# Dynamic convolution's three engine orders laid out anew, and residual tiles loaded and summed beside the sweeps, in a four-layer float32 kernel

## The reference, cut to what matters

```python
x = x + L0(gn(x))   # dynamic 3x3 convolution: mean -> hidden -> softmax gives 4 weights, which mix 4 experts per sample
x = x + L1(gn(x))   # four sweeps (down, up, right, left): row += relu(conv1d(previous row)), 9 taps
x = x + L2(gn(x))   # linear attention with rotation, plus a 3x3 depthwise convolution of a view of the input
x = x + L3(gn(x))   # four sweeps again
```

## Time and profile before

| | us |
|---|---|
| median of 3 runs | 3129.11 |
| the profiled execution | 3132.45 |
| its span | 3130.7 |
| stage one | 0 to 428 |
| first layer's sweeps | 428 to 1339 |
| local stage | 1339 to 1583 |
| attention | 1583 to 2118 |
| third layer's sweeps, final sum | 2118 to 3130.7 |

### The profile page before, as it was taken

One profiled execution on the slowest core, in us unless ns is written; L12 is line 12 of the kernel. 1 busy time (PEld: TensorE's weight loads), 2 busy tenths in 40 slices (PEclk: granted clock), 3 DMA queues, 4 the chain that ended last, 5 costly groups with the idle time before them and its releaser, 6 DMA issues. The chain is left out here.

```text
span 3130.7 us, 71818 instructions
## 1 busy us (share of the span) xinstructions
PE 2747.3 (88%) x25712; PEld 2482.8 (79%) x25712; DVE 2172.1 (69%) x5174; ACT 1363.0 (44%) x2113; POOL 288.4 (9%) x801
## 2 busy tenths in 40 slices
PE   5888879999999999917969998878999999999791
PEld 3666669999999999913447777758999999999791
DVE  7888846666666666687018888886666666666865
ACT  3766642246632222236436666643225662222120
POOL 1112110000000000045000101010000000000602
PEclk9899989999999999958979999998999999999795
DMA  4334230000000000087054877856000000000758
GB/s 89 81 90 99 67 124 0 0 0 0 0 0 0 0 0 0 0 233 198 1 87 73 120 104 102 116 73 107 0 0 0 0 0 0 0 0 0 121 94 127
DMA packets 735622, 164.89 MB, mean 53 GB/s; under 512 B 728209, under 2 KB 728849, under 8 KB 730641
## 3 DMA queue, kind: packets, MB, share of 16 engines
q1 hardware_dynamic: 608928, 136.86, 22.7%
q10 hardware_dynamic: 126576, 26.41, 5.4%
HBM read 96.13 MB, written 67.11 MB: 52 GB/s over the span
## 5 line engine op out<-in xcount | busy, mean ns | idle before, releaser
L269 PE MATMUL L_conv<-L_x_hi,L_w_hi 128*128 128x256 f32 x5040 | 1251.0, 283 | 46.5 <-DVE L_w_lo L236 28.7
L269 PE MATMUL L_conv<-L_x_hi,L_w_lo 128*128 128x256 f32 x5040 | 1249.5, 283 | 0.0
L156 ACT ACTIVATE L_row_b<-S,L_bias 128x256 f32 (+1 forms) x1008 | 514.2, 510 | 1168.9 <-DVE L_x_hi L210 1158.0
L269 PEld LDWEIGHTS L_conv<-L_x_hi,L_w_hi 128*128 128x128 f32 x5040 | 958.7, 190 | 49.5 <-issue 28.9
L269 PEld LDWEIGHTS L_conv<-L_x_hi,L_w_lo 128*128 128x128 f32 x5040 | 957.0, 190 | 0.0
L220 DVE SCALAR_TENSOR_TENSOR S<-L_conv,L_neg_bias,L_row_b 128x256 f32 x1008 | 487.7, 484 | 517.5 <-PE L_conv L273 516.7
L273 PE MATMUL L_conv<-L_x_lo,L_w_hi 128*128 128x256 f32 x5040 | 771.3, 284 | 4.9 <-DVE L_x_lo L212 4.8
L273 PEld LDWEIGHTS L_conv<-L_x_lo,L_w_hi 128*128 128x128 f32 x5040 | 677.7, 190 | 7.4 <-DVE L_x_lo L212 7.4
L212 DVE TENSOR_TENSOR L_x_lo<-S,L_x_hi 128x256 fp32r<-128x256 f32 x1016 | 455.3, 448 | 34.7
L210 DVE TENSOR_SCALAR L_x_hi<-S 128x256 fp32r (+1 forms) x1016 | 316.7, 312 | 35.3
L604 PE MATMUL dc_conv<-dc_xz_hi,dc_w_hi 128*128 128x512 f32 x384 | 171.3, 446 | 6.5 <-DVE dc_w_lo L731 6.5
(11 more groups left out here) (177 smaller groups left out, 2896.4 us busy)
## 6 DMA issues: line engine op xcount, KB each, us to landing
dc_raw<-x SPq DMA_DIRECT2D x32, 512.0 KB, 6.6
x_scratch<-dc_raw SPq DMA_DIRECT2D x16, 1024.0 KB, 7.4
lp_xr<-x_scratch SPq DMA_DIRECT2D x16, 1024.0 KB, 7.0
x_scratch<-lp_xr SPq DMA_DIRECT2D x32, 512.0 KB, 7.7
at_res<-x_scratch SPq DMA_DIRECT2D x32, 512.0 KB, 10.5
x_scratch<-at_res SPq DMA_DIRECT2D x64, 256.0 KB, 5.3
fs_buf<-x_scratch SPq DMA_DIRECT2D x32, 512.0 KB, 6.7
at_G<-x_scratch ACTq DMA_DIRECT2D x56, 256.0 KB, 5.8
```

Source lines behind the costliest of these rows:

```text
L156: nc.scalar.activation(row_b[p][:, :, :], line(k, at_step(k, i), p), ACT.Identity, bias=bias[:, k:k + 1]).then_inc(row_b_ready[p], 1)
L269: nc.tensor.matmul(out, w[:, k, s * P:(s + 1) * P], x_hi[p][:, s:s + J, :], start=(s == 0 and n == 0), stop=False)
```

## The change

Stage one: the orders of TensorE, ScalarE and VectorE in a sample. TensorE does chunk 0 first, then the input group; the hidden product stands behind two thirds of chunk 1, the logits behind a third of chunk 2. VectorE makes the low input of a sample's second part in that sample's own turn, and the first part's behind the mixing weights; the first expert's share is made by ScalarE (`first_expert`). ScalarE's moves into S are issued one by one, the fourth of them two samples late. `beff` has two buffers. The experts' loads move from ScalarE's queue to SP's, behind the first image. At the start mixing is done ahead of the low inputs.

Beside the sweeps: the tiles of the ring now live through sweeps, local stage and attention, where they are G, the rotations, one turned tile and the constants (class `Shared`). SP loads five of them beside the first layer's sweeps. Within the last sweep GpSimd adds three of four quarters of the columns, and VectorE takes their statistics, one between the halves of a step. The local stage adds and measures the fourth quarter of these five samples. The bands are loaded at the start of the local stage, from ScalarE's queue, and waited for in four parts. x2 has the layout [16, 128, 2048] and is stored in one DMA per sample; attention's residual loads become four DMAs for two. Attention's constants and its first two G are loaded by SP at the end of the local stage; of G only the pad columns are set to one. The diff, cut to its core:

```diff
-                with dve.Fori(0, STEPS) as i:
-                    for p in range(2):
-                        step(k, dve.snap(i), p)
+                if k == 3 and final:
+                    final.early_vector(dve, step)
+                else:
+                    with dve.Fori(0, STEPS) as i:
+                        for p in range(2):
+                            step(k, dve.snap(i), p)
...
-            for n in range(PER):
+            load(0, 0)
+            sp.dma_start(ex[0], halves(experts[:, 0, :])).then_inc(ex_in, 16)
+            sp.dma_start(ex_rest[:, :, :], experts[:, 1:KE, :]).then_inc(ex_in, 16)
+            for n in range(1, PER):
                 load(n, n)
             with sp.Fori(0, B // PER - 1) as t:
                 for u in range(PER):
...
-            act.dma_start(ex[0], halves(experts[:, 0, :])).then_inc(ex_in, 16)
-            act.dma_start(ex_rest[:, :, :], experts[:, 1:KE, :]).then_inc(ex_in, 16)
...
+            def first_expert(m):
+                act.wait_ge(weight_ready, m + 1)
+                nc.scalar.activation(w_mix, ex[0], ACT.Identity, scale=weight[:, 0:1]).then_inc(first_mixed, 1)
...
                 n = t * PER + k
                 first, last = isinstance(n, int) and n == 0, isinstance(n, int) and n == B - 1
+                second = isinstance(n, int) and n == 1
                 if not first:
                     evacuate(n * CH - 1, (k - 1) % PER, CH - 1, n - 1)
+                if not first and not second:
+                    to_slot(n - 2, (k - 2) % PER, 1, 1)
                 if not last:
                     centre(t, k + 1, 0)
                 evacuate(n * CH, k % PER, 0, n)
                 if not last:
                     hidden(n + 1)
+                    centre(t, k + 1, 1)
                     exps(n + 1)
-                    centre(t, k + 1, 1)
+                    first_expert(n + 1)
                 evacuate(n * CH + 1, k % PER, 1, n)
+                if not first:
+                    to_slot(n - 1, (k - 1) % PER, 0, 0)
                 if not last:
                     high_weights(n + 1, (k + 1) % 2)
                 if not first:
-                    to_slot(n - 1, (k - 1) % PER, 0)
+                    to_slot(n - 1, (k - 1) % PER, 0, 1)
                 evacuate(n * CH + 2, k % PER, 2, n)
                 if not first:
-                    to_slot(n - 1, (k - 1) % PER, 1)
+                    to_slot(n - 1, (k - 1) % PER, 1, 0)
...
             centre(0, 0, 0)
-            centre(0, 0, 1)
             hidden(0)
             exps(0)
+            act.wait_ge(ex_in, 2 * 16)
+            first_expert(0)
+            centre(0, 0, 1)
             high_weights(0, 0)
             walk(act, sample)
             evacuate(B * CH - 1, B % PER - 1, CH - 1, B - 1)
-            to_slot(B - 1, (B - 1) % PER, 0)
+            to_slot(B - 2, (B - 2) % PER, 1, 1)
+            to_slot(B - 1, (B - 1) % PER, 0, 0)
...
-                if not last:
-                    group(n + 1, INP)
                 products_high(n, 0, u, 0)
                 products_high(n, 0, u, 1)
                 products_low(n, 0, u)
                 if not last:
-                    hid(n + 1)
+                    group(n + 1, INP)
                 products_high(n, 1, u, 0)
                 if not first:
                     group(n - 1, RES)
+                products_high(n, 1, u, 1)
+                if not last:
+                    hid(n + 1)
+                products_low(n, 1, u)
+                products_high(n, 2, u, 0)
                 if not last:
                     logits(n + 1)
-                products_high(n, 1, u, 1)
-                products_low(n, 1, u)
-                for q in range(2, CH):
-                    products_high(n, q, u, 0)
-                    products_high(n, q, u, 1)
-                    products_low(n, q, u)
+                products_high(n, 2, u, 1)
+                products_low(n, 2, u)
+                products_high(n, 3, u, 0)
+                products_high(n, 3, u, 1)
+                products_low(n, 3, u)
...
-                if e == 0:
-                    chain.step(nc.vector.tensor_scalar(w_mix, ex[0], weight[:, 0:1], None, ALU.mult))
-                else:
-                    chain.step(nc.vector.scalar_tensor_tensor(out=w_mix, in0=ex[e], scalar=weight[:, e:e + 1],
-                                                              in1=w_mix, op0=ALU.mult, op1=ALU.add))
+                if e == 1:
+                    dve.wait_ge(first_mixed, m + 1)
+                chain.step(nc.vector.scalar_tensor_tensor(out=w_mix, in0=ex[e], scalar=weight[:, e:e + 1],
+                                                          in1=w_mix, op0=ALU.mult, op1=ALU.add))
...
                 if not last:
                     group_var(n + 1, INP, k + 1)
+                effective_bias(k)
+                remainder(n, k, 1)
                 if not first:
                     result_stats(n * CH - 1, (k - 1) % PER, CH - 1)
-                effective_bias(k)
-                if not first:
                     aggregate("result", RES)
                     squares(RES)
                 if not last:
                     gate_mean(n + 1, k + 1)
-                    remainder(n + 1, k + 1, 0)
                     gate_hidden(n + 1)
                 if not first:
                     group_var(n - 1, RES, k - 1)
...
                 result_stats(n * CH, k % PER, 0)
                 if not last:
                     mixing_weights(n + 1)
-                    for e in range(KE):
-                        mix(n + 1, (k + 1) % 2, e)
+                    remainder(n + 1, k + 1, 0)
                 if not first:
                     result_affine(n - 1, k - 1)
+                if not last:
+                    for e in range(1, KE):
+                        mix(n + 1, (k + 1) % 2, e)
                 result_stats(n * CH + 1, k % PER, 1)
                 if not last:
-                    remainder(n + 1, k + 1, 1)
                     low_weights(n + 1, (k + 1) % 2)
...
             gate_mean(0, 0)
             gate_hidden(0)
+            softmax_in(0)
+            mixing_weights(0)
+            dve.wait_ge(ex_in, 2 * 16)
+            for e in range(1, KE):
+                mix(0, 0, e)
+            low_weights(0, 0)
             remainder(0, 0, 0)
-            softmax_in(0)
-            remainder(0, 0, 1)
             for q in range(CH):
                 input_stats(0, 1, q)
             aggregate("input", INP)
             squares(INP)
-            mixing_weights(0)
-            dve.wait_ge(ex_in, 2 * 16)
-            for e in range(KE):
-                mix(0, 0, e)
-            low_weights(0, 0)
...
-            for pw in range(2):
-                dst, src, scale, shift = slot_move(B - 1, (B - 1) % PER, (B - 1) % 2, 1, pw)
+            for ph, pw in ((0, 1), (1, 0), (1, 1)):
+                dst, src, scale, shift = slot_move(B - 1, (B - 1) % PER, (B - 1) % 2, ph, pw)
...
+    def load(self, eng):
         for g in range(4):
             part = slice(g * 16, g * 16 + 16)
+            eng.dma_start(self.band0[:, part, :], self.source0[:, part, :]).then_inc(self.loaded[g], 16)
+            eng.dma_start(self.band1[:, part, :], self.source1[:, part, :]).then_inc(self.loaded[g], 16)
...
+class Shared:
...
+    def add_quarter(self, eng, n, g):
+        part = slice(g * QUARTER, (g + 1) * QUARTER)
+        cells = self.xr[n][:, :, part]
+        return eng.tensor_tensor(cells, cells, columns_of(self.S, n)[:, :, part], ALU.add)
+
+    def quarter_stats(self, n, g):
+        return self.nc.vector.bn_stats(self.bn[:, n, g, :], self.xr[n][:, :, g * QUARTER:(g + 1) * QUARTER])
+
+    def early_sync(self, sp):
+        for n in range(RING):
+            self.load_residual(sp, n)
+
+    def early_pool(self, pool, new_ready, done_before):
+        for n in range(RING):
+            pool.wait_ge(self.x1_in[n], 16)
+        for g in (3, 2, 1):
+            for p in range(2):
+                pool.wait_ge(new_ready[p], done_before(3, STEPS - g * QUARTER))
+            for n in range(RING):
+                self.add_quarter(self.nc.gpsimd, n, g).then_inc(self.quarter_summed, 1)
+
+    def early_vector(self, dve, step):
+        def several(first, last):
+            with dve.Fori(first, last) as i:
+                for p in range(2):
+                    step(3, dve.snap(i), p)
+
+        at = 0
+        for g in (3, 2, 1):
+            ready = STEPS - g * QUARTER + RING + 1
+            several(at, ready)
+            for n in range(RING):
+                step(3, ready + n, 0)
+                dve.wait_ge(self.quarter_summed, (3 - g) * RING + n + 1)
+                self.quarter_stats(n, g).then_inc(self.early_stats, 1)
+                step(3, ready + n, 1)
+            at = ready + RING
+        several(at, STEPS)
...
                 sp.wait_ge(x2_ready, n + 1)
-                for q in range(2):
-                    sp.dma_start(x2[n].rearrange("c (i q) w -> q c i w", q=2)[q],
```

(39 more changed lines are left out.)

196 lines of the change are left out of this document (114 added, 82 removed).

## The result

The changed kernel takes **3225.76 us** (median of 4 runs, 3223.04 to 3228.18) against 3129.41 (4 runs): ratio **1.0299**, 95% interval 1.0283 to 1.0314. The prediction said 3170, 3116 to 3208: the side was right, the size not. The profiled execution has a span of 3224.0 us (+93.3) and a mean clock of 0.930 (before 0.945).

| stage | before | after | difference | predicted |
|---|---|---|---|---|
| stage one | 429.2 | 508.5 | +79.3 | +61 |
| first layer's sweeps | 910.2 | 918.1 | +7.9 | +13 |
| local stage, to the first tap | 85.6 | 84.9 | -0.7 | -21.3 |
| taps | 156.2 | 156.0 | -0.2 | 0 |
| last tap to the first transpose | 18.5 | 5.4 | -13.1 | -12.4 |

The account below looks back on a forecast made before the run. VectorE, not TensorE, was taken to set stage one's pace. Terms +61 (stage one), +13 (sweep), -21.3 (local stage), -12.4 (attention's start), +0.5 (barrier) sum to +41: 3173 us profiled, 3170 as median; range 3116 to 3208.

Parts of the forecast that it names:

- The loop through chunk 0: Stage one: VectorE's input variance waits for chunk 0, which waits for VectorE's low weights; TensorE idles 3.2 and 4.2 us.
- The clock: Stage one: half clock behind two idles per sample, 1.6 us lost at each, lifting the period from 25.6 to 28.8 us.
- rival 1: Stage one: only the longer idle lowers the clock; 27.2 us per sample, 3147 us; chance 0.18.
- rival 2: Stage one: the clock stays up; 25.6 us per sample, 3120 us, faster than before; chance 0.16.
- Rival 3: Stage one: slow clock through both 4.3 us stretches of products; 32.4 us per sample, 3220 us; chance 0.11.
- Stage one, +61: Whole dynamic convolution: 28.8 us per sample against 24.17, less savings at start and end; +61 us, bounds +15 and +110.
- full-clock step: Stage one laid out at TensorE's full clock: 25.6 us per sample against 24.17, with GpSimd's 3.3 us root covered.
- The sweep, +13: First layer's last sweep: GpSimd's quarter-tile additions slow VectorE, +9 us, and slow clock adds +4; bounds 0 and 31.
- The local stage, -21.3: Local stage: with five tiles mostly prepared, the sixth sample begins after 22.4 us instead of 43.7; -21.3 us to first tap.
- Rival 4: Local stage: bands share queue engines with first stores, sixth tile 10 us late, local gain halves; 3180 us; chance 0.07.
- The attention's start, -12.4: Start of attention: constants and images fetched ahead, only small memsets left, TensorE starts at 1587.2 instead of 1599.66; -12.4 us.
- The attention inside, 0: Inside attention: residual loads as four DMAs move the same bytes, so 0 us.

Follow-up runs that it names:

- group_front: Changed kernel with TensorE's input-statistics group product put back ahead of chunk 0; 3180.60 us, ratio 1.0156.
- fillers: Changed kernel with constant-matrix products in TensorE's two stage-one idles, 14 ahead of the result statistics, 11 ahead of the mixed weights; 3173.18 us, ratio 1.0133.
- lb_first: Changed kernel with lb's load put ahead of the eight band loads on ScalarE's queue; 3206.25 us, ratio 1.0259.
- lb_joints: Changed kernel with the kernel before's dynamic convolution, and lb's load ahead of the bands; 3125.95 us, ratio 0.9985.
- joints_best: Changed kernel with the kernel before's dynamic convolution, lb's load ahead of the bands and x2's old layout and DMAs; 3136.99 us, ratio 1.0023.

## Why the prediction was right or wrong

- **The loop through chunk 0: right.** VectorE's input variance is released by TensorE's group product, both idles are there at 4.1 and 3.0 us (4.2 and 3.2), and group_front takes the one ahead of chunk 0 away.
- **The clock: right in mechanism, its size partly luck.** The fillers give back 3.5 us a sample against the 3.2 of the sum. But the sum had 3.2 us of slow loop work behind each idle, at a half each. Measured are 3.4 us behind the one and mostly 6.8 around the other, 8.5 with TensorE at work, at 0.4 each: the two errors nearly cancel. The stretches behind both idles refute rival 1, the fillers rival 2. Rival 3, slow through both stretches, was nearer for the stretch around the result group, but its 32.4 us a sample is too high (measured 29.95). The prediction also read the Trainium skill (TensorE: Matmul & The Clock Gate, What's actually happening) so that the clock term would be dropped, which made 3120. Dropped so, it fails here: the fillers show 50.4 us, 1.6% of the time. The Trainium skill says there that for modeling the ramp penalty is under 1% of a typical span and that one should not fit a specific count of slow products, in a passage on the warm-up at the start of a kernel; to carry that over to an idle that comes back in every sample was the prediction's step. In the kernel before's stage one, whose slow products are off VectorE's loop, dropping the term costs nothing: filling that idle brought 1.8 us.
- **Stage one, +61 for +79.3: a term mis-sized.** The step that failed is the one at full clock: 25.6 us, measured 26.46. "GpSimd's root takes 3.3 us and is covered" is off: the root takes 5.0 us beside the remainder that was to cover it, and leaves a wait of 0.72 us. The local stage's part of the prediction did count 0.9 us for an addition that holds the root up; the same was left out here. The waits for the group product and the logits are another 0.6 longer, that for the hidden product 0.75 shorter (0.3 I could not place; the turn from which its pieces were read, 204.91 to 228.79 us, is 0.3 shorter than the mean of 24.17, which may be it). That full-clock step and the clock's 0.3 make 1.15 us a sample, 16 of the 18.
- **The sweep, +13 for +7.9: a term mis-sized.** A half-length addition takes 1.6 us (1.5 said), and +9 for the additions came as 7.9; the slow clock (+4) did not come: TensorE's idles of 0.7 us and less left the clock at 1.00.
- **The local stage, -21.3 for -0.7: a step missed**, the largest error. The pace was right (the sixth sample 22.1 us in, but for the wait; 22.4 predicted), but "the band loads come here; see the rivals" looked only at the tiles. lb stands behind the bands on ScalarE's queue, and TensorE's first product waits for it. lb_first gives back 17.2 us in this stage (19.5 in all); the 67.7 us to the first tap are then 3.4 over the 64.3 predicted, by the 2.4 us still waited for that product and the tiles' reloads. Rival 4 had the contention and the wrong victim.
- **The attention's start, -12.4 for -13.1: right.**
- **The attention inside, 0 for +22.3: wrong.** "Residual loads as four DMAs move the same bytes: 0" did not ask how long they take. About 11 us go with the new layout of x2 and its loads (541.4 against 530.2 on average); the clock behind the stalls is 3.4 us at most; the rest is open.

With the local stage and the attention as measured, the sum is +41 + 20.6 + 22.3 = +84, 3213: these two terms alone lead out of the range. The range was too narrow on the upper side because its bounds held stage one's unknowns alone.

## What to carry to other kernels

When a load is moved onto a queue, list every load that the same edit leaves behind it and who waits for each: a wait for "all constants" ends with the last one, however small. When a product is moved behind a block of others, follow its result round the other engines back to that block's own input; if it arrives there, the block has become part of the loop, and so has TensorE's clock. Work that is put beside another engine's chain to cover it can also lengthen that chain. A change of layout is costed at both its ends: here the contiguous store saved 16 us beside the bands (67.6 us to the first tap in lb_joints, 83.4 in joints_best), and the loads behind it lost 11 in the attention (539.7 against 528.5). One sample's window is not the stage: the sample at 341 us shows 3.4 us at the lower clock around an idle where 12 of 14 have 6.8.
